# A routing pipeline cut anew: each batch's gate moved one period ahead, its slots to the period's end, statistics behind the vector engine's chain, and an add behind every routed scatter

## The chip, the cores and the metric

One Trainium2 chip, one of its cores. The metric is the device time of one execution in microseconds (us). The core has a matrix engine (TensorE, PE in the profile; PEld are its weight loads), a vector engine (VectorE, DVE), an activation engine (ScalarE, ACT), GpSimd (POOL), which here issues the indirect DMAs, and the queue engine SyncE (SP).

## The reference

Three blocks run over x of shape (8, 1024, 256), all float32: half a mixture-of-experts block, linear attention, and the same expert block again with the same weights.

```python
x = x + 0.5 * ffn(layernorm(x))
x = x + attention(layernorm(x))
x = x + 0.5 * ffn(layernorm(x))

def ffn(x):                       # 8192 tokens of 256, 16 experts of width 128, 2 shared of 128
    scores = softmax(x @ gate_w.T); orig = scores; scores = scores + gate_b
    # 4 groups of 4; a group's score is the sum of its 2 best; keep 2 groups, then the 2 best experts
    weights = orig at the two chosen
    y = sum over the chosen e: weight_e * ((silu(x @ We1[e] + be1[e]) * (x @ We3[e] + be3[e])) @ We2[e] + be2[e])
    z = (silu(x @ ws1 + bs1) * (x @ ws3 + bs3)) @ ws2 + bs2
    return y + z
```

## The kernel before

The residual stream `xres` stays on chip, 128 partitions by 8 batches by 8 tiles (`NT`) of 256. An expert block (`L` is 0 or 1, `r = 8 * L + b` counts batches over both) has two stages.

**Routing** (`route` in each engine's program) takes one batch per period. For batch r: DVE computes statistics (`stats_work`, L957 to L965), POOL raises the variance to the power -1/2 (`rstd`), DVE forms `nmr` (`negate_mean`, L977), ACT normalises 8 tiles (`normalise`, L748) into one of three buffers `xs`, PE transposes them (`transpose`, L411; four pieces), ACT copies each piece out of its bank (`copy_xT`, L764), PE computes the gate's logits (`gate`, L421), and DVE runs the long serial chain of `route_work`: from the row maximum `mx` (L1027) and the shifted logits `sh` (L1028) over ACT's exponentials (`ex`, L777) to the chosen experts `sel` (L1071) and the `weight` (L1078). PE then counts ranks (`rank`, L479 and L482), DVE turns these into row numbers (`slots`, L993 to L1005), ACT appends the token's data (`meta`), and POOL sends the rows of the batch to `expert_rows` by 16 indirect DMAs (`scatter`, L1388), one for each tile and choice; behind every fourth it adds half a bias to a piece of `xres` (`add_bias`, L1380, from the third batch on). `xs` has three buffers, so `normalise` of batch r+1 waits until the rows of r-2 have been sent.

Beside this, PE computes the shared expert. It is cut into 49 parts: `part_of(n)` says which. An "up" part is 4 matmuls of 512 columns (L444), followed by `silu` on ACT (L772) and `gated` on DVE (L1135); a "down" part is 8 matmuls of 256 columns (L460), followed by two `add_shared` on DVE (L1143). The trace records each of these float32 matmuls as two: 8 records for an up part, 16 for a down part, 32 for a gate. `FIRST[b]` is the first part of period b; parts 37 to 44 (`TAIL`) follow the last period while the tables are made, 45 to 48 (`HELD`) follow the experts. The bank of an up part is taken again two up parts later, once `gated` has read it. On DVE, `work` is a generator: `shared(L, n, work, steps)` runs so many of its steps before it handles part n. Each engine's order is that in which the code is written; engines meet only at semaphores.

**Experts**: 143 tiles (`TILES`) of 128 rows are loaded in turn; PE transposes (L567), multiplies (L576, L586) and adds the bias (L588), ACT and DVE gate (L846, L1224), DVE scales (L1235) and POOL scatters the tile to `routed_rows` (L1416). The 104 remaining bias adds (`BIAS_PARTS`, 128 columns each) stand one each behind the first 104 of these scatters. The semaphore `bias_added`, for which DVE waits before it combines, is raised at the 16th and at the last add.

## Time and profile before

| | |
|---|---|
| median of 3 runs (lowest, highest) | 1455.86 us (1450.14, 1465.67) |
| profiled execution, its span | 1444.71 us, 1443.0 us |
| busy: PE, DVE, ACT, POOL | 1248.3, 923.5, 668.2, 698.3 us |
| mean granted clock of PE | 0.943 of 2.4 GHz |
| stage 25 to 285 us (routing 0): PE, DVE, POOL busy, clock | 237.26, 154.62, 150.45 us, 0.93 |
| stage 885 to 1130 us (routing 1): PE, DVE, POOL busy, clock | 213.26, 145.72, 148.60 us, 0.93 |
| stage 285 to 620 us (mostly experts 0): PE, DVE, POOL busy, clock | 306.43, 229.60, 191.55 us, 0.97 |

In a routing stage a PE that is 90% busy still loses time in three ways: it waits, it runs at half clock for a while after it waited, and some of its matmuls are spread out. Busy shares show none of these; start times do.

### The profile page before, as it was taken

To read this page: it belongs to the slowest core of one execution; us is meant where nothing else is said; L and a number is where in the kernel's file an instruction comes from. 1 tells how busy PE (TensorE), PEld (TensorE's weight loads), DVE (VectorE), ACT (ScalarE), POOL (GpSimd) and SP (SyncE) were. 2 spreads that over 40 slices of the span, in tenths; PEclk is the share of its full clock that TensorE was granted. 3 is DMA by queue.
4 is the path that set the end of the run, shared out by engine and by line. 5 is a ranking of instruction groups with operands and counts; after the bars stand their busy time and mean duration, and the time that the engine had idled before them with its cause. 6 is when DMAs were issued, how large, how long until landed. Compare 5 with 4: busy or idle time off the path is not lost.

```text
span 1443.0 us, 27088 instructions
## 1 busy us (share of the span) xinstructions
PE 1248.3 (87%) x7150; PEld 991.9 (69%) x7150; DVE 923.5 (64%) x3310; ACT 668.2 (46%) x1466; POOL 698.3 (48%) x848
## 2 busy tenths in 40 slices
PE   4998999899999877999999988979869999999830
PEld 3566665699998756878878874646535899998720
DVE  4674856377876556667766646756734677775556
ACT  3344431477776523344434434434411777775500
POOL 2456766488887430000000003467664688885400
PEclk9997999999999997999999998999989999999965
DMA  9521224555554423111110001122224555554389
GB/s 360 184 72 71 78 86 124 156 159 164 158 161 131 131 90 105 59 60 59 58 48 28 1 0 38 56 86 79 71 90 126 149 161 161 159 158 123 92 325 374
DMA packets 92938, 172.78 MB, mean 120 GB/s; under 512 B 17368, under 2 KB 60141, under 8 KB 91507
## 3 DMA queue, kind: packets, MB, share of 16 engines
q1 hardware_dynamic: 63318, 92.98, 21.7%
q0 software_dynamic: 26016, 67.81, 13.2%
q10 hardware_dynamic: 3456, 10.25, 1.8%
q8 instruction: 64, 1.05, 0.3%
q14 instruction: 84, 0.69, 0.2%
HBM read 88.51 MB, written 86.39 MB: 121 GB/s over the span
## 4 chain that ended last, share of the span: by engine, by line
PE 67%; DVE 11%; issue 7%; ACT 5%; DMA 4%; another core or an unknown queue 3%; POOL 3%; SPq 0%; DVEq 0%; ACTq 0%; POOLq 0%
PE bank L576 18%; PE bank L586 9%; PE bank L444 8%; PE bank L460 6%; PE bank L567 4%; PE bank L620 4%; PE bank L609 4%; PE bank L421 3%; PE bank L683 3%; DMA w<-routed_rows 3%; POOL expert_rows L1388 2%; PE bank L588 2%; PE bank L411 2%; ACT xn L853 1%
## 5 line engine op out<-in xcount | busy, mean ns | idle before, releaser
L1416 POOL DMA_INDIRECT routed_rows<-xn,rdest x286 | 282.9, 989 | 137.0 <-DVE rw L1213 77.3
L576 PE MATMUL bank<-rows,att 128*128 128x128 f32 x2288 | 306.8, 278 | 0.1
L576 PEld LDWEIGHTS bank<-rows,att 128*128 128x128 f32 x2288 | 282.4, 194 | 0.8 <-ACT att L841 0.4
L1388 POOL DMA_INDIRECT expert_rows<-rows,slots x192 | 186.9, 974 | 176.2 <-DVE slots L1005 110.3
L1224 DVE SCALAR_TENSOR_TENSOR rows<-bank,tile_b,att 128x128 f32<-128x128 f32 x286 | 100.1, 350 | 155.5 <-ACT att L846 121.3
L841 ACT COPY att<-w 128x512 f32 x286 | 177.9, 622 | 23.2 <-issue 16.5
L586 PE MATMUL bank<-w,rows 128*128 x572 | 173.3, 385 | 16.4 <-DVE rows L1224 15.4
L460 PE MATMUL bank<-ws,work 128*128 128x256 f32 x512 | 143.6, 424 | 25.3 <-DVE work L1135 15.5
L840 ACT COPY rows<-bank 128x256 f32<-128x256 f32 x286 | 106.7, 373 | 78.3 <-PE bank L567 57.8
L460 PEld LDWEIGHTS bank<-ws,work 128*128 128x128 f32 x512 | 103.2, 211 | 53.9 <-DVE work L1135 20.2
L1375 POOL TENSOR_TENSOR rstd<-ve,minus_half 128x8 f32<-128x8 f32 x8 | 13.1, 1640 | 257.3 <-DVE ve L965 257.3
L1235 DVE TENSOR_SCALAR xn<-bank,rw 128x256 f32<-128x256 f32 x286 | 135.8, 475 | 1.7 <-remote 0.9
L846 ACT ACTIVATE att<-bank,tile_b 128x128 f32<-128x128 f32 x286 | 104.8, 367 | 50.7 <-PE bank L576 48.0
L1380 POOL TENSOR_TENSOR xres<-xres,half_bs 128x128 f32<-128x128 f32 x256 | 121.9, 476 | 4.9
L567 PE MATMUL bank<-ident,rows 128*128 128x128 f32 x572 | 111.1, 276 | 6.5 <-DMA rows<-expert_rows 4.8
L772 ACT ACTIVATE silu<-bank,bs 128x512 f32<-128x512 f32 x64 | 43.6, 686 | 151.2 <-PE bank L444 73.0
L567 PEld LDWEIGHTS bank<-ident,rows 128*128 128x128 f32 x572 | 72.0, 143 | 42.4 <-issue 6.2
L586 PEld LDWEIGHTS bank<-w,rows 128*128 128x128 f32 x572 | 87.0, 192 | 20.3 <-issue 20.0
L444 PE MATMUL bank<-xn,ws 128*128 128x512 f32 x192 | 93.1, 628 | 3.5 <-DVE work L1135 2.5
L444 PE MATMUL bank<-xnT,ws 128*128 128x512 f32 x192 | 93.7, 613 | 1.0 <-issue 1.0
L1143 DVE SCALAR_TENSOR_TENSOR xres<-bank,xres 128x512 f32<-128x512 f32 x64 | 44.2, 691 | 76.8 <-PE bank L460 42.0
L588 PE MATMUL bank<-bias_rows,ones 128*128 x286 | 78.3, 274 | 0.0
(184 smaller groups left out, 2185.6 us busy)
## 6 DMA issues: line engine op xcount, KB each, us to landing
rows<-expert_rows SPq DMA_DIRECT2D x286, 130.5 KB
rows<-routed_rows SPq DMA_DIRECT2D x32, 512.0 KB, 4.2
w<-routed_rows SPq DMA_DIRECT2D x10, 1024.0 KB, 18.6
out<-xres ACTq DMA_DIRECT2D x16, 512.0 KB, 7.2
xres<-in_x SPq DMA_DIRECT2D x7, 1024.0 KB, 9.4
rows<-routed_rows SPq DMA_DIRECT2D x6, 1024.0 KB, 15.2
expert_rows<-pad SPq DMA_DIRECT2D x47, 130.5 KB
routed_rows<-xn,rdest POOLq DMA_INDIRECT x286
```

The lines of the kernel that those rows point to most:

```text
L444: last = nc.tensor.matmul(bank[:], ws[:, c, mi * P:(mi + 1) * P], xnT[:, c, g * HALF:(g + 1) * HALF], start=c == 0, stop=c == KC - 1)
L460: last = nc.tensor.matmul(y_ps[j][:, t % 2 * C:(t % 2 + 1) * C], m.gT[:, g, mi, t * P:(t + 1) * P], m.ws2[:, mi, :], start=mi == 0, stop=m ...
L567: last = nc.tensor.transpose(rT_ps[a % 2][:, c * P:(c + 1) * P], m.rin[:, a % SLOTS, c * P:(c + 1) * P], m.ident[:])
L576: last = nc.tensor.matmul(rh_ps[t % RB][:, n * P:(n + 1) * P], m.rw13[:, t % RB, c * C + n * INTER:c * C + (n + 1) * INTER], m.rT[:, t % R ...
L586: nc.tensor.matmul(ry_ps[y % RB][:, 0:C], m.rgT[:, y % RB, :], m.w2[:, bass.ds(e, C)], start=True, stop=False)
L588: nc.tensor.matmul(ry_ps[y % RB][:, 0:C], m.ones3[:], m.bias_rows[:, BE2:BE2 + E * C][:, bass.ds(e, C)], start=False, stop=True).then_inc( ...
L840: nc.scalar.copy(m.rT[:, a % RB, :], rT_ps[a % 2][:, 0:C]).then_inc(s.rT_copied, 1)
L841: nc.scalar.copy(m.rw13[:, a % RB, :].rearrange("p (c n) -> p c n", c=KC), w13[:, :, bass.ds(expert_at(i + 2), C)]).then_inc(s.rw13_copied, 1)
L1235: nc.vector.tensor_scalar(m.ry[:, n, :], ry_ps[y % RB][:, 0:C], m.rw[:, n:n + 1], None, ALU.mult).then_inc(s.ry_scaled, 1)
L1380: return nc.gpsimd.tensor_tensor(x, x, m.half_bs2[:, c:c + P], ALU.add)
L1388: nc.gpsimd.indirect_dma_start(out=d.xg, out_offset=bass.IndirectOffsetOnAxis(ap=m.slots[:, b % XS, k, i:i + 1], axis=0), in_=xs[:, i, :], ...
L1416: nc.gpsimd.indirect_dma_start(out=d.yt, out_offset=bass.IndirectOffsetOnAxis(ap=m.rdest[:, n:n + 1], axis=0), in_=m.ry[:, n, :], in_offse ...
```

## The change

PE: the gate of batch r+1 is computed in period r, two tiles behind each quarter of the period's last part, and the rank of r is taken after the first two pairs; in period 0 all 8 tiles follow the rank at once. Period 0 keeps 2 parts in place of 5, and periods 1 to 7 hold 5 each (`FIRST`). DVE: `slots(r)` is run in period r, ahead of the last part's work, not in period r+1; `stats_work(r + 2)` comes after `weight` (for r = 0 it stays ahead of the chain, for r = 8 it stays behind the slots), `negate_mean(r + 2)` at the end of the period. ACT: `exponentials(r)` comes ahead of `normalise(r + 1)`. POOL: `rstd(r + 3)` comes behind all 16 scatters of r, not between them. Experts: the 104 adds become 143, 65 of 128 columns and 78 of 64, one behind each scatter.

```diff
-FIRST = (0, 5, 9, 14, 18, 23, 27, 32, 37)
+FIRST = (0, 2, 7, 12, 17, 22, 27, 32, 37)
...
-BIAS_PARTS = [(b, i, c) for b in reversed(range(BATCHES)) for i in range(NT) for c in (0, P)
-              if b >= BATCHES - 2 or i >= 4 or c]
+REST = [(b, i, c) for b in reversed(range(BATCHES)) for i in range(NT) for c in (0, P)
+        if b >= BATCHES - 2 or i >= 4 or c]
+WIDE = 2 * len(REST) - TILES
+BIAS_PARTS = [(b, i, c, P) for b, i, c in REST[:WIDE]] + [(b, i, c + h, 64) for b, i, c in REST[WIDE:] for h in (0, 64)]
...
                         for j in range(4):
                             transpose(r + 1, j)
                         rank(r)
-                        for j in range(n + 2, FIRST[1]):
-                            shared(L, j)
+                        gate_tiles(r + 1, range(NT))
                         continue
-                    shared(L, n, gate_pair)
-                    shared(L, n + 1)
-                    shared(L, n + 2, first_half)
-                    shared(L, n + 3, second_half)
-                    if n + 4 < FIRST[b + 1]:
-                        shared(L, n + 4)
-                    rank(r)
+
+                    def transposes(at):
+                        return lambda j: transpose(r + 1, at[j]) if more and j in at else None
+
+                    def gates(j):
+                        if more:
+                            gate_tiles(r + 1, (2 * j, 2 * j + 1))
+                        if j == 1:
+                            rank(r)
+
+                    n = FIRST[b]
+                    shared(L, n)
+                    shared(L, n + 1, transposes({1: 0}))
+                    shared(L, n + 2, transposes({1: 1, 3: 2}))
+                    shared(L, n + 3, transposes({1: 3}))
+                    shared(L, n + 4, gates)
...
                     n = FIRST[b]
-                    if more:
+                    if b == 0:
                         normalise(r + 1)
-                    if b == 0:
                         exponentials(r)
...
+                    exponentials(r)
+                    if more:
+                        normalise(r + 1)
                     shared(L, n)
-                    exponentials(r)
...
             def route_work(r):
                 b = r % BATCHES
-                if b > 1:
-                    yield from slots(r - 1)
-                if b + 2 < BATCHES and r != BATCHES:
+                if r == 0:
                     yield from stats_work(r + 2)
...
-                if b + 2 < BATCHES and r != BATCHES:
+                if r == 0:
                     negate_mean(r + 2)
-                yield
+                elif b + 2 < BATCHES and b:
+                    yield from stats_work(r + 2)
...
-                        for j in range(n + 2, FIRST[1]):
-                            shared(L, j, iter(()), 0)
                         if L:
                             negate_mean(r + 2)
                         continue
-                    shared(L, n, work, (3 if b > 1 else 0) + (5 if b + 2 < BATCHES else 0) + 1)
-                    others = FIRST[b + 1] - n - 1
-                    for j in range(others):
-                        shared(L, n + 1 + j, work, 17 // others + 1)
+                    shared(L, n, work, 6)
+                    for j in range(1, 4):
+                        shared(L, n + j, work, 5)
                     for _ in work:
                         pass
+                    for _ in slots(r):
+                        pass
+                    shared(L, n + 4, iter(()), 0)
+                    if b + 2 < BATCHES:
+                        negate_mean(r + 2)
...
                     if r == BATCHES:
                         rstd(r + 2)
-                    elif b + 3 < BATCHES:
-                        rstd(r + 3)
                     scatter(r, 1)
-                    if r == BATCHES:
+                    if b + 3 < BATCHES:
                         rstd(r + 3)
...
-                    if i < len(BIAS_PARTS):
-                        last = add_bias(BIAS_PARTS[i])
-                    if i in (2 * NT - 1, len(BIAS_PARTS) - 1):
+                    last = add_bias(BIAS_PARTS[i])
+                    if i in (2 * NT - 1, TILES - 1):
                         last.then_inc(s.bias_added, 1)
```

PE in block 0, from the last matmul of the rank of batch 0. Before (the rows stand for parts 2, 3 and 4 and the first half of part 5, into which the gate of batch 1 is woven):

```order
L482 MATMUL bank<-sel,ones_b 128x16
L444 MATMUL bank<-xn,ws 128x512 x4
L460 MATMUL bank<-ws,work 128x256 x8
L444 MATMUL bank<-xn,ws 128x512 x4
L444 MATMUL bank<-xnT,ws 128x512
L421 MATMUL bank<-gate_w,xnT 128x16 x4
L444 MATMUL bank<-xnT,ws 128x512
L421 MATMUL bank<-gate_w,xnT 128x16 x4
```

The same place in the changed kernel:

```order
L485 MATMUL bank<-sel,ones_b 128x16
L424 MATMUL bank<-gate_w,xnT 128x16 x16
L447 MATMUL bank<-xn,ws 128x512 x4
L463 MATMUL bank<-ws,work 128x256 x4
L413 MATMUL bank<-ident,att 128x128 x4
L463 MATMUL bank<-ws,work 128x256 x4
```

The gate of batch 1 has moved ahead of three parts, and the transposes of batch 2 (`ident,att`) into the second of them.

DVE in block 1, first period, behind the slots of batch 8. Before:

```order
L1005 CAST slots<-slot_f 128x16
L957 BN_STATS stat<-xres 128x6 x8
L963 BN_AGGR mv<-stat 128x2 x8
L965 TENSOR_SCALAR ve<-mv 128x8
L1135 SCALAR_TENSOR_TENSOR work<-bank,bs,silu 128x512
L1143 SCALAR_TENSOR_TENSOR xres<-bank,xres 128x512 x2
L1135 SCALAR_TENSOR_TENSOR work<-bank,bs,silu 128x512
L977 SCALAR_TENSOR_TENSOR nmr<-mv,rstd 128x8
```

The same place in the changed kernel:

```order
L1001 CAST slots<-slot_f 128x16
L953 BN_STATS stat<-xres 128x6 x8
L959 BN_AGGR mv<-stat 128x2 x8
L961 TENSOR_SCALAR ve<-mv 128x8
L973 SCALAR_TENSOR_TENSOR nmr<-mv,rstd 128x8
L1020 TENSOR_REDUCE mx<-bank 128x8
L1021 TENSOR_TENSOR sh<-bank,mx 128x128
```

The work of three parts no longer stands between the statistics and `nmr`, whose operand `rstd` comes from POOL, and the chain of batch 9 (`mx`) stands behind it.

POOL at the end of the experts stage. Before:

```order
L1416 DMA routed_rows<-xn,rdest 16384x256
L1380 TENSOR_TENSOR xres<-xres,half_bs 128x128
L1416 DMA routed_rows<-xn,rdest 16384x256
L1380 TENSOR_TENSOR xres<-xres,half_bs 128x128
L1416 DMA routed_rows<-xn,rdest 16384x256 x39
```

The same place in the changed kernel (its last rows):

```order
L1375 TENSOR_TENSOR xres<-xres,half_bs 128x64
L1409 DMA routed_rows<-xn,rdest 16384x256
L1375 TENSOR_TENSOR xres<-xres,half_bs 128x64
L1409 DMA routed_rows<-xn,rdest 16384x256
L1375 TENSOR_TENSOR xres<-xres,half_bs 128x64
```

The 39 scatters that stood without an add between them now have one each.

## Rows read from the trace of the kernel before

**Rows 1.** The page's first line.

```profile
span 1443.0 us, 27088 instructions
```

**Rows 2.** Timeline of PE, 167 to 174 us: start, duration, group; one period's kinds of work.

```profile
167.77 0.96 PE L421 MATMUL bank<-gate_w,w_att 128*128 128x16 f32 x8
168.58 3.70 PE L460 MATMUL bank<-ws,work 128*128 128x256 f32 x16
172.12 1.02 PE L444 MATMUL bank<-xnT,ws 128*128 128x512 f32 x2
172.98 0.60 PE L411 MATMUL bank<-ident,rows 128*128 128x128 f32 x4
173.41 1.88 PE L444 MATMUL bank<-xnT,ws 128*128 128x512 f32 x4
```

**Rows 3.** Timeline of PE: first matmul of ranks 0, 7, 8 and 15.

```profile
46.01 0.22 PE L479 MATMUL bank<-sel,before 128*128 128x144 bf16 x1 [0.77 <-ACT xnT L764]
...
231.69 0.23 PE L479 MATMUL bank<-sel,before 128*128 128x144 bf16 x1
...
881.68 0.30 PE L479 MATMUL bank<-sel,before 128*128 128x144 bf16 x1 [1.14 <-DVE sel L1071]
...
1086.93 0.23 PE L479 MATMUL bank<-sel,before 128*128 128x144 bf16 x1
```

**Rows 4.** Timeline of DVE: chain's start and end in period 2; `nmr` in period 8.

```profile
87.30 0.29 DVE L1028 TENSOR_TENSOR sh<-bank,mx 128x128 f32<-128x128 f32 x1
...
99.63 0.29 DVE L1071 TENSOR_TENSOR sel<-chosen 128x128 bf16<-128x128 f32 x1
...
897.83 0.17 DVE L977 SCALAR_TENSOR_TENSOR nmr<-mv,rstd 128x8 f32<-128x8 f32 x1 [0.66 <-POOL rstd L1369]
```

**Rows 5.** Timeline of ACT, one period's start: normalise, and the silu behind it.

```profile
190.34 4.04 ACT L748 ACTIVATE rows<-xres,nmr,rstd 128x256 f32<-128x256 f32 x8 [7.88 <-DMA expert_rows<-rows,slots]
...
197.31 0.69 ACT L772 ACTIVATE silu<-bank,bs 128x512 f32<-128x512 f32 x1
```

**Rows 6.** Timeline of POOL: an `rstd`; first scatter and last add of batch 6.

```profile
149.27 1.67 POOL L1369 TENSOR_TENSOR rstd<-ve,minus_half 128x8 f32<-128x8 f32 x1
...
217.10 0.98 POOL L1388 DMA_INDIRECT expert_rows<-rows,slots  x1 [3.49 <-issue]
...
238.20 0.47 POOL L1380 TENSOR_TENSOR xres<-xres,half_bs 128x128 f32<-128x128 f32 x1
```

**Rows 7.** Timeline of routing 1: PE down part behind a gate, DVE, later PE wait.

```profile
947.94 0.92 PE L460 MATMUL bank<-ws,work 128*128 128x256 f32 x2
...
960.49 0.29 DVE L1027 TENSOR_REDUCE mx<-bank 128x8 f32<-128x128 f32 x1 [13.63 <-remote]
...
1080.61 6.48 PE L460 MATMUL bank<-ws,work 128*128 128x256 f32 x16 [10.24 <-DVE work L1135]
```

**Rows 8.** Windows of 10 us with and without adds: PE, PEld, DVE, ACT, POOL busy, clock, DMA, GB/s.

```profile
440.00:450.00 10.00, 10.00 (x81) 9.13 (x80) 6.88 (x37) 7.61 (x19) 8.90 (x13) 1.00 0.49 139
...
490.00:500.00 10.00, 8.93 (x69) 7.95 (x68) 6.51 (x36) 6.21 (x17) 5.43 (x6) 1.00 0.41 124
```

**Rows 9.** Timeline of the experts: scatters 1, 105, 143 of block 0; 1, 143 of block 1.

```profile
280.31 1.01 POOL L1416 DMA_INDIRECT routed_rows<-xn,rdest  x1 [15.29 <-DVE rw L1213]
...
453.11 0.99 POOL L1416 DMA_INDIRECT routed_rows<-xn,rdest  x1 [0.17 <-issue]
...
477.43 0.97 POOL L1416 DMA_INDIRECT routed_rows<-xn,rdest  x1 [0.30 <-issue]
479.42 0.37 ACT L846 ACTIVATE att<-bank,tile_b 128x128 f32<-128x128 f32 x1 [4.04 <-PE bank L576]
...
525.57 0.97 POOL L1416 DMA_INDIRECT routed_rows<-xn,rdest  x1 [0.30 <-issue]
...
1127.36 1.01 POOL L1416 DMA_INDIRECT routed_rows<-xn,rdest  x1 [14.05 <-DVE rw L1213]
...
1373.54 0.97 POOL L1416 DMA_INDIRECT routed_rows<-xn,rdest  x1 [0.30 <-issue]
```

More of the change, by code:

```diff
@@ L1377, in add_bias @@
             def add_bias(part):
[L1378 to L1380 removed]
+                b, i, c, width = part
+                x = m.xres[:, b, i, c:c + width]
+                return nc.gpsimd.tensor_tensor(x, x, m.half_bs2[:, c:c + width], ALU.add)
             def scatter(r, k):
```

28 lines of the change are left out of this document (6 added, 22 removed).

## The prediction

> **What bounds the kernel now.** I read the page first: the span is 1443.0 us [rows 1] of an execution of 1444.71, and PE is busy for 87% of it, so the question is where PE is not at work, or works slowly. The timeline of PE in a routing stage gives the price of each piece by its starts [rows 2]: two tiles of a gate 168.58 - 167.77 = 0.81 us, so a gate 3.24; a down part 172.12 - 168.58 = 3.54; a quarter of an up part 0.86, so 3.44; a piece of transposes 0.43, so 1.72 for four. A rank is nine short matmuls, of which the first takes 0.22 [rows 3]; I take 0.6. The reader should then compare this with the distance of the ranks [rows 3]: from rank 0 to rank 7 pass 185.7 us, from rank 8 to rank 15 pass 205.3. In either stretch PE has parts 2 to 36 (35 of them), 7 gates, 6 transposed batches and 7 ranks: 35 x 3.48 + 22.7 + 10.3 + 4.2 = 159 us. So 27 and 46 us are lost in the two stages, and the second stage, which has the same code, is 19.6 longer.
>
> The timelines of the others tell what the loss is. DVE's chain from `sh` to `sel` took 99.63 - 87.30 = 12.3 us with the shared work in it [rows 4], and it starts only when the gate, woven into the period's first part, is over, and the statistics ahead of it in DVE's order too. ACT normalises for 4.04 us, in the row shown after a wait of 7.88 for the rows of an earlier batch, and its `silu` follows only at 197.31, 2.9 after the end of that, because exponentials and two changes of table stand between [rows 5]. POOL needs 238.20 + 0.47 - 217.10 = 21.6 us for a batch's 16 scatters and 4 adds, and 1.67 for an `rstd`, some 1.9 with its gap [rows 6].
>
> A third loss is stranger. In period 11 the down part behind the gate starts at 947.94, so the logits were complete by then, but DVE's `mx`, which waits for nothing else, starts at 960.49, marked with an unknown releaser [rows 7]. PE's next part could not start before either: 960.49 - 947.94 - 3.54 = 9.0 us were lost. PE's wait of 10.24 us at 1080.61, in period 15, has such late signals ahead of it too [rows 7]. These two, 19.2 us, are the whole difference between the stages. I call them late signals. The second also shows the clock: the down part behind it took 6.48 us in place of 3.70 [rows 2, 7], the ratio of the lower level (1.2 GHz) to 2.4.
>
> In the experts stage PE is full while POOL has an add behind each scatter, and 89% busy when it has none [rows 8]. Scatter 105, the first with no add behind it, starts at 453.11 [rows 9]: until then a tile took (453.11 - 280.31) / 104 = 1.66 us, behind it (525.57 - 453.11) / 38 = 1.91. The late signal is seen here at close range: ACT's `att` waited 4.04 us for PE matmuls that the trace had long ended, and came 1.0 us after the end of a run of scatters that stood shoulder to shoulder, the last at 477.43 [rows 9].
>
> **The change, part by part.**
>
> *Order of the periods.* No matmul is added: the parts are spread 2, 5, 5, ... where they were 5, 4, 5, 4, .... A full period holds 5 x 3.48 + 3.24 + 1.72 + 0.6 = 23.0 us of PE [rows 2]. Its rivals for the pace: POOL with 21.6 + 1.9 = 23.5 [rows 6]; DVE with the chain of 12.3, which holds two or three of the seven or so pieces of shared work of 0.7 each, so some 21 with all of them, the statistics and the slots [rows 4]. DVE now finds its logits ready at the start of the period, and its statistics no longer stand before the chain. ACT costs something: `ex` at about 1.0 us into the period, normalising 4.04, a change of table (half of the 2.9 [rows 5], 1.3), then `silu`, over at 7.1; `gated` is over at 7.8, while PE wants that bank at 3.44 + 3.44 + 0.43 = 7.3. So PE waits some 0.5 twice, and I take 24.0 a period, between 23.5 (POOL alone) and 25.5.
>
> *Block 0.* The gate of batch 1 follows rank 0 at once: the first full period starts at 46.0 + 0.6 + 3.2 = 49.8. Rank 7 comes 15.6 us (four and a half parts) into the seventh: 49.8 + 6 x 24.0 + 15.6 = 209.4, where it was 231.7: 22.3 us won. Behind it nothing is added. POOL, from some 49 us (three behind rank 0), needs 8 x 21.6 and five `rstd` of 1.9, so it is free at 231, ahead of PE's tail.
>
> *Block 1, and a wait that the change makes.* `negate_mean(10)` stands directly behind the statistics of batch 10. Its operand comes from POOL, where `rstd(10)` stays behind eight scatters, and it was there at 897.83 [rows 4]. Queued behind it on DVE are the chain of batch 9 and every `gated`; behind that on ACT the exponentials, with `normalise(10)` and two `silu`; behind those PE's transposes, which stand in the middle of part 3. So PE, which has reached them by 890 to 894, goes on at about 901, and the period ends 3.5 parts, 1.72, 3.24 and 0.6 later, at 919. Five periods and 15.6 more: rank 15 at 1055, where it was 1086.9: 32 us won in spite of the stall of 9 [rows 3].
>
> *Late signals.* The 54 us are without them. I cannot name their cause; they come while POOL scatters, and POOL scatters as much as before, but its pauses between batches (3.49 us [rows 6]) shrink. I give back 19.2 us [rows 7] in each block, 38 together; the bounds are 0 and, from the rows, 9.0 in each of twelve steady periods, 108.
>
> *`rstd` behind all scatters* costs nothing: 10 us later on POOL, but its statistics come later too, and `nmr` is wanted only at the period's end. *Slots at the period's end*: the rows can go up to a part's length earlier; the cover is POOL's own backlog.
>
> *Adds.* POOL gets 39 more instructions a block. With 0.98 for a scatter and at most 0.47 for an add [rows 6] it stays under 1.66 a tile. If the pace with adds holds to the end, 38 x 0.245 = 9.3 us are won in block 0, and 1373.54 - 1127.36 - 142 x 1.66 = 10.2 in block 1 [rows 9], 19.5 together. What follows the last scatter in either block waits for it, so all of this shows. The bounds are 19.5 won, and 39 x 0.245 x 2 = 19 lost, if an add of 64 columns is too short to keep signals in time, so that the slow stretch begins at tile 66.
>
> Does the extra work slow DVE? DVE's 37 instructions took 6.88 us with adds beside them, and 36 took 6.51 without [rows 8]: 0.005 us each, hidden in 30% of idle time. The Trainium skill (GPSIMD Engine Reference, Specifications) says that GpSimd's access to SBUF is shared with VectorE and contends with instructions that read two SBUF inputs. By that rule the adds would cost DVE time; by the rows they cost it nothing that PE sees.
>
> On the clock the Trainium skill (TensorE: Matmul & The Clock Gate, HAM oscillation) says that recurring idle gaps keep the array at its lower clock. By the rows a wait of 10 us did it [rows 7]; my 0.5 twice a period would not, and the sum has no term for it.
>
> **Sum.** 1444.7 - 54 + 38 - 19.5 = 1409, and the median of the runs lies 11.2 us above the profiled execution: 1420.
>
> **Rivals.** (1) The late signals return only in part, since PE no longer has its gate at the start of a period: half of them gives 1401, none 1382. For it: block 0 had few; against: nothing shows that the gate causes them. (2) Short adds don't hold the pace, routing gains 16: 1440, and 1459 if the slow stretch doubles. (3) Routing gains nothing, because `normalise` still waits for the rows of three batches back, as it did for 7.88 us [rows 5], and POOL's 23.5 with a landing is the true period; the adds alone give 1436. (4) Slower: late signals follow POOL's pauses. They vanish now, and a tight chain hands every one of them on. With 9.0 us in each of twelve periods, 108 - 54 - 19.5 = 34 us are added: 1490. It decides from (54 + 19.5) / 12 = 6.1 us a period. For it speaks that the longer late signals stand in busy stretches of POOL; against it, that most batches before had none. (5) Nothing moves: 1456.
>
> **How the numbers follow.** Forecast 1420 (1403 to 1433): 0.45. Rival 1: 0.17. Rival 2: 0.14. Rival 3: 0.11. Rival 4: 0.07. Rival 5: 0.06. About 1%, or 15 us, is what a measurement of this kernel can tell from no change. Below 1441 lie the forecast, rival 1, two thirds of rival 2 and most of rival 3: 0.79; within 1% 0.13; slower 0.08. The range reaches into rival 1 at the bottom and over rivals 2 and 3 at the top: 1388 to 1447.
>
> **What would show it.** In the profile of the changed kernel: ranks 1 to 7 some 24 us apart, rank 7 near 209 to 228; in block 1 a DVE that waits some 9 us for `rstd` ahead of `nmr`, and PE idle before the first transposes of batch 10; a steady 1.66 us from scatter 1 to scatter 143; and for the late signals, `mx` or `silu` rows with an unknown releaser. The prediction is wrong if the periods are 26 or more, or if gaps of 3 us return behind tile 66.

## The result, and the profile after

The changed kernel took 1495.26 us (median of 4 runs, 1491.84 to 1501.62); the kernel before, run beside it, 1459.53 (1450.14 to 1465.67). The ratio is 1.026, with a 95% interval of 1.019 to 1.033: slower beyond the noise (by how much more or less than 2% the interval leaves open), where 1420 was forecast. The profiled execution took 1501.62 us. The first two lines of its page answer to [rows 1]:

```profile
span 1499.9 us, 27165 instructions
...
PE 1261.8 (84%) x7150; PEld 996.5 (66%) x7150; DVE 934.6 (62%) x3310; ACT 660.3 (44%) x1466; POOL 716.7 (48%) x926
```

The span grew by 56.9 us, and the two timelines can be laid side by side. The timeline of PE after the change, first matmul of ranks 0, 1, 5, 6, 7, 8 and 15, as in [rows 3]:

```profile
45.96 0.22 PE L482 MATMUL bank<-sel,before 128*128 128x144 bf16 x1 [0.77 <-ACT xnT L762]
82.91 0.22 PE L482 MATMUL bank<-sel,before 128*128 128x144 bf16 x1
...
206.25 0.22 PE L482 MATMUL bank<-sel,before 128*128 128x144 bf16 x1
237.40 0.22 PE L482 MATMUL bank<-sel,before 128*128 128x144 bf16 x1
257.06 0.23 PE L482 MATMUL bank<-sel,before 128*128 128x144 bf16 x1
...
910.21 0.30 PE L482 MATMUL bank<-sel,before 128*128 128x144 bf16 x1 [0.99 <-DVE sel L1064]
...
1127.35 0.23 PE L482 MATMUL bank<-sel,before 128*128 128x144 bf16 x1
```

Rank 7 is 25.4 us later than before, and ranks 8 to 15 take 217.1 us in place of 205.3. The first two periods are 37.0 and 34.3 long, the next four 27.3 to 31.2, where I had 24.0. POOL's timeline of the experts, scatters 1, 66 and 143 of block 0, then 1 and 143 of block 1, as in [rows 9]:

```profile
305.15 1.01 POOL L1409 DMA_INDIRECT routed_rows<-xn,rdest  x1 [15.96 <-DVE rw L1208]
...
413.28 1.00 POOL L1409 DMA_INDIRECT routed_rows<-xn,rdest  x1 [0.17 <-issue]
...
556.12 1.00 POOL L1409 DMA_INDIRECT routed_rows<-xn,rdest  x1 [0.17 <-issue]
...
1176.32 1.01 POOL L1409 DMA_INDIRECT routed_rows<-xn,rdest  x1 [16.15 <-DVE rw L1208]
...
1428.10 1.00 POOL L1409 DMA_INDIRECT routed_rows<-xn,rdest  x1 [0.17 <-issue]
```

The experts take 251.0 and 251.8 us between first and last scatter, where it was 245.3 and 246.2. Until scatter 66 a tile takes 1.66 us, behind it, with the adds of 64 columns, (556.12 - 413.28) / 77 = 1.86. In the windows of 10 us, which answer to [rows 8], PE is full first and then is not (columns: PE, PEld, DVE, ACT, POOL busy, clock, DMA, GB/s):

```profile
345.00:355.00 10.00, 10.00 (x81) 9.14 (x80) 7.47 (x37) 7.49 (x19) 8.84 (x12) 1.00 0.58 163
...
425.00:435.00 10.00, 9.29 (x72) 8.19 (x70) 5.79 (x30) 4.87 (x13) 6.98 (x11) 1.00 0.43 124
```

So the 56.9 are: 25.4 to rank 7, 5.7 and 5.6 in the two experts stages, 11.9 in the second routing up to its last rank, 8.5 from there to the first scatter of its experts, and -0.2 for the rest together. Compared by medians the loss is 36, since the profiled execution of before lay 14.8 us below its median and this one 6.4 above.

What fills a period of 31 us is seen between ranks 5 and 6 (timelines of PE, ACT, DVE and POOL, 209 to 240 us):

```profile
220.30 0.63 PE L413 MATMUL bank<-ident,rows 128*128 128x128 f32 x4 [0.44 <-issue]
...
222.91 0.63 PE L413 MATMUL bank<-ident,rows 128*128 128x128 f32 x4 [0.27 <-issue]
223.38 1.89 PE L463 MATMUL bank<-ws,work 128*128 128x256 f32 x8
230.10 0.68 PE L413 MATMUL bank<-ident,rows 128*128 128x128 f32 x4 [4.83 <-issue]
230.57 3.57 PE L463 MATMUL bank<-ws,work 128*128 128x256 f32 x8
...
222.18 0.59 ACT L762 COPY xnT<-bank 128x512 f32<-128x512 f32 x1 [1.44 <-PE bank L413]
229.37 0.59 ACT L762 COPY xnT<-bank 128x512 f32<-128x512 f32 x1 [6.60 <-remote]
...
232.26 0.69 DVE L1136 SCALAR_TENSOR_TENSOR xres<-bank,xres 128x512 f32<-128x512 f32 x1 [4.98 <-remote]
...
209.16 1.04 POOL L1383 DMA_INDIRECT expert_rows<-att,slots  x1 [6.93 <-DVE slots L1001]
...
229.43 0.96 POOL L1383 DMA_INDIRECT expert_rows<-att,slots  x1 [0.30 <-issue]
```

The third group of transposes was over at 223.54. ACT, idle, starts its copy at 229.37, 5.8 later, and the row's releaser is unknown. PE stands for 4.83, and the 8 records behind it take 3.57 in place of 1.89: the clock has fallen to its lower level (1.2 GHz; granted 0.51 from 230.5 to 234, 1.00 from 223.5 to 230). DVE's `add_shared`, whose matmuls were over at 225.27, starts at 232.26, 7.0 later. The signals were sent in the second half of POOL's sixteen scatters, and arrive about when the last of them ends (230.39). This is the late signal of [rows 7], in nearly every period. ACT's copies of the transposes waited 86.4 us in all for unknown releasers, in 17 places; before, 11.2 in 5. Late signals were not rare before, though: with DVE's rows and ACT's others, waits for unknown releasers between ranks 0 and 7 add up to 32 us before and 84 after, between ranks 8 and 15 to 74 before and 73 after (my sums over both timelines). In block 1 it is not their sum that grew. They stand in eight of these fourteen periods before and in eleven after.

### The profile page after: what moved, and what is told of

It is laid out like the page before. It is cut to its first block, busy times and chain, and to the rows that moved or that the text cites. A ratio compares the mean times of both kernels' runs of the same rounds, so it can differ in the third digit from the quotient of the medians.

```text
span 1499.9 us, 27165 instructions
## 1 busy us (share of the span) xinstructions
PE 1261.8 (84%) x7150; PEld 996.5 (66%) x7150; DVE 934.6 (62%) x3310; ACT 660.3 (44%) x1466; POOL 716.7 (48%) x926
## 4 chain that ended last, share of the span: by engine, by line
PE 63%; DVE 9%; issue 9%; ACT 6%; DMA 5%; another core or an unknown queue 3%; POOL 3%; SPq 1%; ACTq 0%; DVEq 0%; POOLq 0%
PE bank L574 16%; PE bank L447 8%; PE bank L584 8%; PE bank L565 5%; PE bank L463 5%; PE bank L618 4%; DMA w<-routed_rows 4%; PE bank L607 4%; PE bank L424 4%; PE bank L681 3%; POOL expert_rows L1383 2%; PE bank L413 2%; PE bank L586 2%; ACT rows L746 1%
## 5 line engine op out<-in xcount | busy, mean ns | idle before, releaser
L837 ACT COPY att<-w 128x512 f32 x286 | 178.8, 625 | 24.3 <-issue 17.3
L463 PE MATMUL bank<-ws,work 128*128 128x256 f32 x512 | 133.5, 409 | 13.1 <-DVE work L1128 10.4
L1375 POOL TENSOR_TENSOR xres<-xres,half_bs 128x128 f32<-128x128 f32 (+1 forms) x334 | 137.7, 412 | 6.8
L463 PEld LDWEIGHTS bank<-ws,work 128*128 128x128 f32 x512 | 100.1, 203 | 41.0 <-DVE work L1128 17.3
L565 PE MATMUL bank<-ident,rows 128*128 128x128 f32 x572 | 111.3, 277 | 13.0 <-DMA rows<-expert_rows 9.7
L413 PE MATMUL bank<-ident,rows 128*128 128x128 f32 x192 | 36.1, 320 | 79.6 <-issue 38.3
L447 PE MATMUL bank<-xnT,ws 128*128 128x512 f32 x192 | 97.5, 644 | 0.0
L447 PE MATMUL bank<-xn,ws 128*128 128x512 f32 x192 | 96.2, 646 | 1.0 <-DVE xres L1284 1.0
## 6 DMA issues: line engine op xcount, KB each, us to landing
rows<-routed_rows SPq DMA_DIRECT2D x6, 1024.0 KB, 18.4
```

The lines of the kernel that those rows point to most:

```text
L447: last = nc.tensor.matmul(bank[:], ws[:, c, mi * P:(mi + 1) * P], xnT[:, c, g * HALF:(g + 1) * HALF], start=c == 0, stop=c == KC - 1)
L463: last = nc.tensor.matmul(y_ps[j][:, t % 2 * C:(t % 2 + 1) * C], m.gT[:, g, mi, t * P:(t + 1) * P], m.ws2[:, mi, :], start=mi == 0, stop=m ...
L565: last = nc.tensor.transpose(rT_ps[a % 2][:, c * P:(c + 1) * P], m.rin[:, a % SLOTS, c * P:(c + 1) * P], m.ident[:])
L837: nc.scalar.copy(m.rw13[:, a % RB, :].rearrange("p (c n) -> p c n", c=KC), w13[:, :, bass.ds(expert_at(i + 2), C)]).then_inc(s.rw13_copied, 1)
L1375: return nc.gpsimd.tensor_tensor(x, x, m.half_bs2[:, c:c + width], ALU.add)
```

## The experiments

Each ran beside the kernel before on the same chip, and ratios are against that. `pause()` is an idle add on GpSimd: 128 columns of `half_bs2` added to themselves, into a tile that nobody reads, 0.41 us. "Distance" is the mean from one routing scatter's start to the next within a batch, worked out from POOL's timeline as (16th - 1st) / 15.

| run | routing scatters | experts' last 39 | us | ratio (95%) |
|---|---|---|---|---|
| e1_adds | order of before | narrow adds | 1471.8 | 1.003 (0.998-1.007) |
| e2_routing | as changed | as before | 1480.4 | 1.009 (1.005-1.013) |
| e3_pauses | pause behind each | narrow adds | 1457.0 | 0.999 (0.995-1.003) |
| e4_wide | as changed | pauses | 1458.9 | 1.001 (0.996-1.006) |
| e5_both | pause behind each | pauses | 1422.6 | 0.981 (0.976-0.985) |
| e6_before_both | order of before, pause behind each | pauses | 1442.4 | 0.994 (0.991-0.997) |
| e7_short | 32-column pause behind each | pauses | 1399.2 | 0.965 (0.961-0.969) |
| e8_second | pause behind every second | pauses | 1390.3 | 0.960 (0.955-0.965) |
| e9_grouped | the same, behind 4 | pauses | 1403.5 | 0.962 (0.956-0.969) |
| e10_before_second | order of before, every second | pauses | 1409.7 | 0.968 (0.961-0.975) |
| e11_experts_second | every second | every second | 1423.3 | 0.977 (0.970-0.984) |
| e12_early_rstd | every second | pauses | 1401.4 | 0.962 (0.957-0.967) |
| e13_by_eight | the same, behind 8 | pauses | 1411.7 | 0.972 (0.963-0.981) |
| e14_by_sixteen | the same, behind 16 | pauses | 1523.3 | 1.048 (1.037-1.058) |
| e15_small_dose | 32-column pause behind every fourth | pauses | 1431.8 | 0.986 (0.977-0.996) |
| e16_memset | memset behind every second | memsets | 1469.0 | 1.012 (1.001-1.023) |
| e17_rstd_behind | order of before, `rstd` moved | as before | 1514.9 | 1.038 (1.029-1.048) |
| e18_middle | as changed, break in the middle | narrow adds | 1438.4 | 0.989 (0.981-0.996) |

**The two halves of the change, and whether pauses let signals through.** e1 is the kernel before with the new list of adds, e2 the changed kernel with the old list. e3 adds pauses to the routing, e4 to the experts:

```diff
                     if b >= 2 and i % 4 == 3:
                         add_bias((b - 2, 2 * k + i // 4, 0, P))
+                    else:
+                        pause()             # e3
...
                     if i < len(BIAS_PARTS):  # e4: the old list
                         last = add_bias(BIAS_PARTS[i])
+                    else:
+                        pause()
```

> The kernel before with only the new list of bias adds (143 adds in each experts stage, the last 78 of them 64 columns wide). Theory 'a short add is too short': the slow stretch begins with the first narrow add, at tile 66, where it began at tile 105; at the milder pace seen in the changed kernel (some 1.75 us a tile in place of 1.66 and 1.91) 39 tiles lose 0.09 each and 38 win 0.16 each, per block: 5 us faster in all, ratio 0.995 to 1.0. Rival 'adds are a net loss': the routing's rewrite is innocent and the adds carry most of the 36 us: ratio 1.01 to 1.025. Rival 'adds hold the pace': 19.5 us faster, ratio 0.987.

> The changed kernel with the old list of bias adds (104 adds of 128 columns in each experts stage), so that only the routing stage differs from the kernel before. Theory: the routing stage carries the whole loss, so ratio 1.025 to 1.03 against the kernel before. Rival 'the adds carry it': ratio near 1.0.

> The changed kernel, with an idle GpSimd add of 128 columns (into a tile that nobody reads) behind each routing scatter that has no bias add behind it. Theory 'late signals': while scatters stand shoulder to shoulder, PE's signals reach ACT and DVE late, some 5 to 7 us once a period; a pause behind each scatter lets them through. Then the waits of 6.6 us before the third copy of the transposes vanish, POOL's own work grows by about 14 x 0.36 = 5 us a batch to some 28, and that becomes the period: ranks 27 to 28 us apart where they are 31, and 12 x 3 = 36 us less: about 1460. Rival 'it is the order of ACT's and PE's work': POOL's pauses change nothing but make its batches longer: 1495 or more, ranks 31 apart or further, the wait of 6.6 still there.

> The changed kernel, with the adds of the experts stage as before (104 of 128 columns), and an idle add of 128 columns behind each of the last 39 routed scatters. Theory 'the pause behind a scatter has to be long enough': all 143 tiles take 1.66 us, the experts stages lose their slow stretch, and the kernel is 19.5 us faster than the changed kernel with the old list, and 10 to 15 faster than the changed kernel as it is. Rival 'the slow stretch has another cause, such as the rows that are written out': the pace still falls at some tile beyond 100, and nothing is won.

By medians e1 lost 11.5 us and e2 20.0, together near the 35.7 of the whole; the ratios are smaller (e1's interval holds 1.0), and neither theory had them. That the new adds are a loss, not 5 us won, is seen in the trace: e1's experts stages take 252.2 and 252.9 us against 245.3 and 246.2, its tiles 67 to 105 1.90 us each, and the last 38 still 1.85. The routing does not carry everything either. In e4 the pace is 1.66 to scatter 105 and 1.69 behind it, 21 us under e2, where 19.5 was expected, and 36 under the changed kernel, where 10 to 15 was. e3's time went as its first theory had it: 38 us under the changed kernel, though POOL has 208 more instructions. In its trace no wait of ACT's copies or DVE's chain has an unknown releaser; what is left of "remote" there is 3.4 us in the whole run. Its ranks are not 27 to 28 apart, as expected, but 24.1 to 30.5.

**Do they add up, how long, how often?** e5 joins e3 and e4; e6 does so in the kernel before; e7 has `pause(32)` in the routing, e8 `elif i % 2: pause()`.

> The changed kernel with both kinds of idle adds: behind each routing scatter that has no bias add, and behind each of the last 39 routed scatters of an experts stage (the bias adds there 104 of 128 columns, as before). If the two gains are of one cause and add up: the routing gains 38 us as in the run with pauses in the routing alone, the experts stages 29 us as between narrow adds (1.88 and 1.85 us a tile) and wide ones (1.66 and 1.69): 1457 - 29 = 1428, ratio 0.978. Rival 'it is one fixed amount of loss that moves elsewhere': no better than either alone, 1455.

> The kernel before with the same idle adds in both stages. It tells what the new order of the periods is worth once signals are on time. Theory 'GpSimd's batch, 26.4 us with the pauses, is then the period under either order': within 10 us of the changed kernel with both, about 1430. Rival 'the new order is better by its own': its periods stay near 28, and it is 15 to 30 us slower than the changed kernel with both, 1445 to 1458.

> As the changed kernel with both kinds of idle adds, but the idle adds of the routing stages are 32 columns wide in place of 128 (those of the experts stages stay at 128). Theory 'a pause has to be long enough, as with the 64 columns in the experts stage': the waits with unknown releaser come back in part, periods are 28 or more, 1440 to 1455. Rival 'any instruction between two scatters does': POOL's batch shrinks by 12 x 0.25 = 3 us to 24, periods are 24 to 25, and the time is some 1400.

> As the changed kernel with both kinds of idle adds, but in the routing a pause or a bias add stands behind every second scatter only. Theory 'what counts is how long the run of scatters shoulder to shoulder is': two in a row delay a signal by less than 2 us, POOL's batch is 24, periods are 25: 1410 to 1420. Rival 'every gap is needed': late waits as long as in the changed kernel, periods of 28 or more, 1445 or more.

The gains add up (1422.6, where 1428 was expected). e6 lies between its two cases. e7's first theory fell: a pause of 0.25 us is enough in the routing. e8 came out below its range of 1410 to 1420. With POOL's batch short again, some periods of the changed kernel are what I had forecast. PE in e8, ranks 5 and 6 and the transposes between them:

```profile
172.47 0.22 PE L481 MATMUL bank<-sel,before 128*128 128x144 bf16 x1
...
181.99 0.66 PE L412 MATMUL bank<-ident,rows 128*128 128x128 f32 x4 [0.25 <-ACT rows L745]
...
186.52 0.63 PE L412 MATMUL bank<-ident,rows 128*128 128x128 f32 x4 [0.44 <-ACT xnT L761]
...
188.71 0.60 PE L412 MATMUL bank<-ident,rows 128*128 128x128 f32 x4
...
190.87 0.60 PE L412 MATMUL bank<-ident,rows 128*128 128x128 f32 x4
191.31 1.89 PE L462 MATMUL bank<-ws,work 128*128 128x256 f32 x8
...
196.46 0.22 PE L481 MATMUL bank<-sel,before 128*128 128x144 bf16 x1
```

23.99 us, with PE waiting 0.25 and 0.44, and the clock at 2.4 GHz (granted 1.00 from 177 to 201). Rank 7 stands at 216.45, 40.6 earlier than in the changed kernel. It is the fastest kernel of the study: 4.0% under the kernel before.

Not every period is 24, though hardly a signal is late. From rank 3 to rank 5 e7 takes 30.2 and 29.3 (e9 30.9 and 29.3, e12 28.9 and 29.1). PE in e7 (143 to 146 us), and the window of 10 us around it (columns as above):

```profile
145.15 1.22 PE L462 MATMUL bank<-ws,work 128*128 128x256 f32 x2 [2.85 <-DVE work L1127]
...
142.00:152.00 10.00, 7.15 (x26) 6.13 (x26) 6.43 (x25) 1.70 (x4) 8.80 (x15) 0.63 0.24 86
```

PE waits for `gated`, which stands on DVE behind the end of the chain and two of the new statistics, and then runs at its lower clock for a part of two periods (granted 0.63 in this window, 0.50 in the next, 0.84 in the one after). In e8 the wait in this place is 2.48, its releaser isn't found, the clock stays at 1.00 from 140 to 170, and the periods are 25.6 and 24.3.

**Run length or mean distance; the order alone; the experts; the stall.** e9 has e8's instructions to the last one, behind each fourth scatter. e10 is the kernel before with e8's pauses. e11 leaves out every second pause in the experts. e12 puts `rstd(10)` behind four scatters of batch 8.

> The same instructions as in the run with a pause or an add behind every second routing scatter (1390 us), but grouped: four scatters in a row, then both adds one behind the other. POOL's work for a batch is the same to the instruction (23.4 us), only the runs of scatters are four long again. Theory 'what counts is the length of the run': the waits with unknown releaser come back, periods of 28 to 31, 1430 to 1450. Rival 'what counts is the mean distance of the scatters, 1.46 us in place of 1.36': waits stay away, periods of 24.0, 1385 to 1395.

> The kernel before with a pause or an add behind every second routing scatter, and idle adds behind the last 39 routed scatters. It prices the change of order alone, with signals on time and with POOL's batch (23.4 us) shorter than PE's period. Theory: the new order reaches 24.0 a period and the old one some 26, so this is 12 x 2 = 24 us or more slower than the 1390 of the changed kernel with the same pauses: 1412 to 1425. Rival 'the order is worth nothing, it was the late signals alone': 1385 to 1400.

> The changed kernel with the pauses behind every second scatter in the routing, and in the experts stages too the idle add stands behind every second only of the last 39 routed scatters. Theory 'runs of two are harmless everywhere': the pace stays at 1.66 to 1.69 a tile, 1385 to 1395. Rival 'in the experts stage POOL's cycle must not be shorter than 1.6 us' (1.52 with an add of 64 columns was too short): the pace falls to 1.8 or 1.9 from tile 105 on, 8 to 17 us more: 1398 to 1407.

> The changed kernel with pauses behind every second scatter, and rstd(10) on POOL behind the fourth scatter of batch 8 in place of the eighth. DVE waited 10.16 us for it ahead of nmr, ACT and PE behind that (PE 4.98 before the first transposes of batch 10). Theory: POOL gives it 5.8 us earlier, DVE's wait falls to some 4.5, PE's goes, and the kernel is 5 us faster, 1385. Rival 'normalise is over too late anyway' (4.0 us of it and a change of table stand behind it): nothing, 1390.

Runs of four are harmless if the distance is right (1.41 to 1.46 in e8 and in e9, batch 8 with its `rstd` aside), against the first theory of e8 and e9. The order is worth little by itself: e10 lies 6 to 8 us above e9 and e12, which were measured with it, and e6 20 above e5; the 24 or more that I expected of e10 did not come. In e11 the pace fell to 1.95 from scatter 106 on (446.91 to 519.15 for 37 scatters), the rival's case, though with 20 us over e9 it cost more than its 8 to 17: so in the experts a POOL cycle of 1.42 is too short, which in the routing it is not. e12's stall shrank as meant, DVE's wait for `rstd` from 10.16 to 4.47, and nothing came of it. Rank 9 stood 34.8 behind rank 8 (38.1 in e8 and e7), but rank 10 another 29.0 (23.8), so the rival's time was right: given back a period later, where PE waits 2.95 us for `gated` and the clock is at 0.50 from 896 to 906.

**Over what stretch, how much, and what kind of instruction.** e13 and e14 group the same instructions behind eight and sixteen scatters, e15 has only a `pause(32)` behind each fourth, e16 a memset for the idle add.

> The same instructions as with a pause or add behind every second routing scatter (1390 us, ratio 0.960), in groups: eight scatters in a row, 1.27 us apart, then the two adds and two idle adds. Theory 'the distance counts as a mean over a dozen microseconds or more': like groups of four, ratio 0.96. Rival 'the scatters leave a backlog of about 0.1 us or more each, which delays a signal once it has grown over some eight scatters': late waits return within each half batch, ratio 0.97 to 0.98.

> As before, with all sixteen scatters of a batch in a row (20.3 us) and then the four adds and four idle adds. POOL's work for a batch is still the same. Theory of a mean over a whole period: ratio 0.96. Theory of a backlog that grows while scatters are 1.27 us apart: signals late by 5 us or more at the end of each batch, as in the changed kernel, periods near 31: ratio 1.0 or more.

> The changed kernel with a 32-column idle add (0.25 us) behind every fourth routing scatter, behind the bias add where there is one: distances of 1.43 us where there is an add, and 1.34 in the first two batches; the experts stages with idle adds behind the last 39 scatters. If the limit in the routing lies between the 1.37 of the changed kernel and 1.43, as the run with 32-column pauses behind every scatter says: ratio 0.965. If four adds' worth of pause is not enough: ratio 0.98 to 1.0.

> The changed kernel with pauses behind every second routing scatter and behind the last 39 routed scatters, where each idle instruction is a memset (it writes 128 columns and reads nothing) in place of an add. Theory 'any instruction that keeps the next scatter away does': as with adds if it lasts as long, ratio 0.96 to 0.965; if it is much shorter than 0.4 us, the experts stages fall back to 1.9 a tile and the ratio is 0.97 to 0.98, while the routing stays at periods of 24. Rival 'it is the reading of SBUF by the add': late waits in the routing as in the changed kernel, ratio 1.0.

The backlog theory has its forecasts right in both. In e14, POOL's sixteen scatters start 1.27 apart from 192.50 to 211.54 (timelines of POOL, PE and ACT):

```profile
192.50 1.04 POOL L1386 DMA_INDIRECT expert_rows<-rows,slots  x1 [8.40 <-DVE xres L1135]
...
198.68 0.60 PE L412 MATMUL bank<-ident,rows 128*128 128x128 f32 x4
...
201.07 0.58 ACT L761 COPY xn<-bank 128x512 f32<-128x512 f32 x1
...
203.45 0.60 PE L412 MATMUL bank<-ident,rows 128*128 128x128 f32 x4
...
211.54 0.96 POOL L1386 DMA_INDIRECT expert_rows<-rows,slots  x1 [0.30 <-issue]
...
215.26 0.59 ACT L761 COPY xn<-bank 128x512 f32<-128x512 f32 x1 [13.61 <-remote]
215.99 0.45 PE L412 MATMUL bank<-ident,rows 128*128 128x128 f32 x1 [10.21 <-ACT xn L761]
```

The transposes that ended at 199.28 were copied as soon as ACT was free; those that ended at 204.05 were copied 11.2 later, 2.8 behind the end of the last scatter. It is the same work on every engine, and some 120 us more than e9. e15 shows the dose inside one run. PE, ranks 0 to 3:

```profile
45.92 0.22 PE L481 MATMUL bank<-sel,before 128*128 128x144 bf16 x1 [0.77 <-ACT xnT L761]
82.84 0.22 PE L481 MATMUL bank<-sel,before 128*128 128x144 bf16 x1
117.52 0.22 PE L481 MATMUL bank<-sel,before 128*128 128x144 bf16 x1
141.52 0.22 PE L481 MATMUL bank<-sel,before 128*128 128x144 bf16 x1
```

While batches 0 and 1 are scattered, without bias adds and 1.32 apart, periods take 36.9 and 34.7; with batches 2 to 5, at 1.39 to 1.41, 24.0 to 25.7. In the changed kernel these are 1.29 apart (periods 36.9, 34.3) and 1.35 to 1.38 (27.3 to 31.2). So the distance from which periods are short again lies about 1.4. e15's ratio falls short of the 0.965 mostly by the periods in which batches 0, 1 and 9 are scattered: against e8 they lose 7.6, 10.6 and 8.8 us. e16 gave neither of its cases cleanly: a memset lasts 0.23 and starts without the gap that an add has, so the distance was 1.37 to 1.38 beside bias adds, hardly more than in the changed kernel, and next to nothing was won in the routing (periods 25 to 37 until the last). That fits distance; whether the reading of SBUF (the chip's working memory, where the tiles are) plays a part as well, it can't tell.

**Where the distance was lost.** In the trace of before, the batches that have bias adds and an `rstd` between their halves (2 to 4) have distances of 1.46 to 1.47, those with adds alone (5 and 6) 1.35 and 1.34; batches 0 and 1, with an `rstd` and no adds, 1.55 and 1.40. The change moved that `rstd`. e17 is the kernel before with that alone:

```diff
                     scatter(r, 0)
                     if r == BATCHES:
                         rstd(r + 2)
-                    elif b + 3 < BATCHES:
-                        rstd(r + 3)
                     scatter(r, 1)
-                    if r == BATCHES:
+                    if b + 3 < BATCHES:
                         rstd(r + 3)
```

e18 is the changed kernel with a break put back:

```diff
                     scatter(r, 0)
                     if r == BATCHES:
                         rstd(r + 2)
+                    else:
+                        for _ in range(4):
+                            pause()
                     scatter(r, 1)
```

> The kernel before with one part of the change: rstd(r+3) stands behind all sixteen scatters of batch r in place of between its halves. The mean distance of the scatters in batches 0 to 4 falls from 1.40-1.55 to 1.28-1.35 us. Theory 'the break in the middle let the signals through': periods 2 to 5 grow by some 3 us each in block 0 (in block 1 by as much), ratio 1.01 to 1.02. Rival 'rstd's place costs nothing', as the prediction held: ratio 1.0 (0.995 to 1.005).

> The changed kernel with nothing but four idle adds (some 2 us in all, as long as an rstd with its gaps) between the two halves of each batch's scatters in the routing, except in batch 8, where an rstd stands there already; its adds in the experts stages stay as they are. Theory: a break behind eight scatters is nearly as good as one behind every second, as in the run with groups of eight (ratio 0.972 with the experts' pauses, which are worth some 0.02): ratio 0.99 to 1.0, ranks 24 to 28 us apart, against 1.026 without the break. Rival 'four adds a batch are too little': ratio 1.015 or more.

e17 cost more than I expected: one instruction of 1.67 us moved in four or five batches of a block costs 3.8%, some 55 us, more than the whole change. Its distances fell to 1.28 and 1.27 in batches 0 and 1 and 1.35 to 1.36 in 2 to 4. Its ranks (timeline of PE: 0, 1, 2, 6 and 7, then 8 and 15):

```profile
46.03 0.28 PE L479 MATMUL bank<-sel,before 128*128 128x144 bf16 x1 [0.77 <-ACT xnT L764]
84.22 0.22 PE L479 MATMUL bank<-sel,before 128*128 128x144 bf16 x1
120.25 0.23 PE L479 MATMUL bank<-sel,before 128*128 128x144 bf16 x1
...
233.87 0.23 PE L479 MATMUL bank<-sel,before 128*128 128x144 bf16 x1
278.87 0.23 PE L479 MATMUL bank<-sel,before 128*128 128x144 bf16 x1
...
922.97 0.30 PE L479 MATMUL bank<-sel,before 128*128 128x144 bf16 x1 [1.09 <-DVE sel L1071]
...
1155.48 0.23 PE L479 MATMUL bank<-sel,before 128*128 128x144 bf16 x1
```

Rank 7 is 47.2 us later than in the kernel before [rows 3]. Of this, 18.4 come in the first two periods, in which batches that lost their break are scattered, and 22.9 in the last, in which batch 6 is, and its distance is as before. What is new there is that no gap parts it from batch 5 (0.17 us, where it was 3.49 [rows 6]): 32 scatters run from 219.79 to 262.95 with nothing but the bias adds between them, and DVE's `mx` waits (timelines of POOL and DVE):

```profile
241.88 0.99 POOL L1388 DMA_INDIRECT expert_rows<-rows,slots  x1 [0.17 <-issue]
...
265.65 0.29 DVE L1027 TENSOR_REDUCE mx<-bank 128x8 f32<-128x128 f32 x1 [25.46 <-remote]
```

The gate for which it waits was over at 244.49, 21.2 earlier. In this order of work a late `rstd` can also hold DVE up directly; its waits for it add up to 9.8 us in both blocks, so that is the smaller part at most. And e18, four idle adds in every batch but batch 8 and nothing else, turns the changed kernel from 2.6% slower into 1.1% faster; ranks 1 to 3 stand at 71.10, 95.22 and 119.21. It is the cleaner of the two tests, though it also parts batches 5, 6 and 7, which no `rstd` had parted before.

## Why the prediction was wrong

Between the profiled executions 35.5 us were to be won, and 56.9 were lost. Of the 92.4 between them, 53.3 are in the two routings up to the last rank (16 to be won, 37.3 lost), 30.8 in the adds (19.5 to be won, 11.3 lost) and 8.3 elsewhere, mostly between rank 15 and its experts.

**The step that failed** is the sentence that moving `rstd` behind all scatters costs nothing. I counted its time on POOL and when its result is wanted, and both were right: in the changed kernel no `nmr` but that of batch 10 waits for it. What it did besides was to part two runs of eight scatters; without it signals of PE come late in eleven of fourteen periods in place of eight, and by more in block 0 (84 us of such waits in place of 32). e18, which puts a break back and nothing else, shows that, and e17 shows what the move costs by itself.

**Late signals, 19.2 us a block.** The term was taken from two places of block 1 and given back unchanged, with the remark that POOL scatters as much as before. As much, but closer together. Measured as the distance of the changed kernel to those with pauses that take them away, they cost 39.8 us from rank 0 to rank 7 and 30.1 from rank 8 to rank 15 (e8), or 31.6 and 35.0 (e7), or 30.7 and 26.3 (e9): 57 to 70 for both, where 38 had been given back. The upper bound of that term, 9.0 in each of twelve periods, made rival 4: 1490 against a measured 1495. Its mechanism, "late signals follow POOL's pauses", and its place in nearly every period were right; that its number fits is luck, since it has the adds winning 19.5 and the order 54. I gave it 0.07, because most batches before had none. That was a misreading: waits for unknown releasers stand in eight of fourteen periods of the trace of before. And ten of its sixteen batches were parted by an `rstd`, which the rows of POOL would have shown.

**The period of 24.0** is there in part when signals are on time: 23.99 between ranks 5 and 6 of e8, and 24.0 to 24.1 in two or three of the first six periods of e7, e9 and e18 too. Even in e8 rank 7 is at 216.45 rather than 209.4, since the first period is 29.3 and the fourth 25.6. In e7, e9 and e12 two periods are 29 to 31, by the wait of 2.85 for `gated` and the half clock behind it, for which the sum had no term. So the gain over the old order was over-sized: against the kernel before, e7, e8, e9 and e12 win 20 to 33 us between ranks, not 54. In block 1 that is the late signals of the old order alone: with them gone e10 takes 182.5 us from rank 8 to rank 15, as little as e7 (182.2). In block 0 pauses hardly move the old order (183.9 in e10, 185.7 before), and the new one wins 3.5 to 12.6 on it (e9, e8). With pauses in both, the new one is 6 to 20 us ahead in all (e10, e6).

**Short adds.** The forecast of 19.5 us won took the pace to hold; its other bound, a slow stretch from tile 66 at 19 lost, had the place right. Lost were 11.3, since the pace was 1.86, not 1.91. (In the sum won, the 10.2 of block 1 comes to 10.5 with the 1.66 written there.) What the runs rank by is how soon POOL can start the next scatter, its cycle: 1.60 (wide pauses) holds 1.69 a tile, 1.52 (64 columns) gives 1.86, 1.42 (e11) 1.95, 1.27 (none, before) 1.91 [rows 9]. The last two are out of order, so it is not the cycle alone. That adding an instruction to 38 bare scatters helps was right; that any add will do was wrong.

**The stall for `rstd(10)`** was forecast as some 9 us and is there: DVE's row, and PE's behind it:

```profile
926.40 0.17 DVE L973 SCALAR_TENSOR_TENSOR nmr<-mv,rstd 128x8 f32<-128x8 f32 x1 [8.98 <-POOL rstd L1364]
...
929.58 0.66 PE L413 MATMUL bank<-ident,att 128*128 128x128 f32 x4 [3.64 <-ACT att L746]
```

PE lost 3.64 of it, not 9, though the period came out as forecast (36.6 between ranks 8 and 9; 919 less 881.7 is 37.3). e12 shows that shortening the stall brings nothing in the end.

**DVE beside the adds.** I took 0.005 us each from two windows. In e3 DVE is busy for 956.3 us against 934.6 with 208 more idle adds, 0.10 each, but in e18, with 60, for only 928.3, so there is no steady price. The rule in the Trainium skill (GPSIMD Engine Reference, Specifications), that instructions with two SBUF inputs contend with GpSimd for SBUF, is borne out in kind (`prod`, two instructions: 0.72 us in e3 at 182.89, where POOL's add starts at 182.84; 0.49 in the rows without one). It was hidden, as I said, since DVE waits a third of the time.

**The clock.** The two short waits a period left it at 2.4 GHz (e8), as forecast. The late signals' waits of 4.8 did not (3.57 for 1.89), and neither did the one of 2.85 in e7. The rule of the Trainium skill that I set aside (TensorE: Matmul & The Clock Gate, HAM oscillation), that recurring idle gaps bring the lower clock back, agrees with these rows, and to leave it out of the sum was wrong even where signals are on time.

## What to carry to other kernels

When an instruction is moved, ask not only what waits for it but what it keeps apart: on a queue that issues indirect scatters back to back, a 1.7 us instruction between two runs of eight was worth 3.8% of this kernel. Where consumers start late with an unknown releaser while GpSimd scatters, measure the distance of the scatters first, and try idle instructions between them before rewriting the order of the work: 158 of 0.41 us (e8) brought more (4.0%) than any reordering here. Look across batches too: a gap of 3.5 us between two runs that closes makes one long run of them. And a term that is read from two places of the trace of before is a property of those places' neighbours; look at what the batches without it have in common.

## What the runs showed of the hardware

PE's signals to ACT and DVE can arrive 5.8 (changed kernel) to 21.2 us (e17) late while GpSimd issues indirect scatters 1.27 to 1.36 us apart, and the delay grows with the length of the run: none to be seen for a signal sent 6.8 us into the run of e14, 11.2 us for one sent 11.5 into it. In e14 and e17 the held signals came 2.8 and 2.7 us behind the end of the last scatter.

PE itself can be held up too. Behind the gate of [rows 7], the records of the down part that starts at 947.94 stand about 1.4 us apart (PE in the kernel before, 948 to 960 us, the second of them):

```profile
950.50 0.38 PE L460 MATMUL bank<-ws,work 128*128 128x256 f32 x1 [1.64 <-issue]
```

PE's next part starts at 960.57, so this one took 12.6 us in place of 3.54, with the clock granted at 0.72. The 9.0 us that the prediction read there as PE waiting for its next part were lost inside this part. Why the records stand apart, no run shows.

At a mean of 1.42 and more between the routing's scatters, in groups of up to four, little of the delay is left between the ranks (waits for unknown releasers under 3 us a block in e7 and e8, 11 in e9); at 1.40 (e15) some of up to 5.7 us stay, at places where they cost the periods little (24.0 to 25.7 in block 0); in groups of eight more is left (e13, e18). Behind rank 7 of e8, with a DMA share of 0.78 from 225 to 250 us, ten such waits, 22 us together, are back at a distance of 1.43. The limit is not sharp: the late `mx` of [rows 7] came with a batch whose mean was 1.46, in two runs of eight. In the experts stages, where each scatter has a load of rows beside it (DMA share 0.49 and 0.58 in the full windows of [rows 8] and above, against 0.19 to 0.28 in the changed kernel's routing windows 126 to 150, 176 to 206 and 209 to 229 us), 1.60 was enough and 1.52 was not. The DMA engines are far from full in both. What is held up inside the chip, and why PE's signals, no run here shows. All pauses thin out the issuing on GpSimd and the traffic of the rows alike, and no run issued the same scatters in another way, so the two are not parted. Nor was it tried to put the `rstd` back between the halves in the changed kernel, whose statistics would come too late for it there.
